# The first part of a fused attention and feed-forward kernel, rescheduled step by step

## The reference

```python
x = x + matmul(fake_quant(layernorm(x)), fake_quant(ctx))            # "L0": 8-bit levels, float result
x = x + ffn(layernorm(x))       # h @ W.T + b + LoRA mixed by a router over the mean of rows 179..510
x = x + attention(layernorm(x), ctx)     # 32 query heads, 8 key/value heads, rope, softmax, output product
x = x + ffn2(layernorm(x))      # h @ W_up.T + top-1 expert LoRA
```

## Time and profile before

| | |
|---|---|
| median of 3 runs | 2168.59 us (2164.77 to 2170.65) |
| the profiled execution | 2167.87 us, its span 2166.1 us |
| mean granted TensorE clock | 0.983 |
| busy share of the span | PE 95%, PEld 71%, DVE 72%, ACT 46%, POOL 37% |
| chain that ended last | PE 84%, DVE 7%, DMA 3%, issue 2% |

### The profile page before, as it was taken

One profiled execution on the slowest core, in us unless ns is written; L12 is line 12 of the kernel. 1 busy time (PEld: TensorE's weight loads), 2 busy tenths in 40 slices (PEclk: granted clock), 3 DMA queues, 4 the chain that ended last, 5 costly groups with the idle time before them and its releaser, 6 DMA issues.

```text
span 2166.1 us, 25646 instructions
## 1 busy us (share of the span) xinstructions
PE 2058.2 (95%) x9176; PEld 1539.6 (71%) x9176; DVE 1563.3 (72%) x2861; ACT 986.9 (46%) x1402; POOL 802.2 (37%) x521
## 2 busy tenths in 40 slices
PE   6999798899979999999999999999999999998799
PEld 5777575777846777777777777677777777776587
DVE  3874588646457888878888788778787878787343
ACT  3222122231146555555555555555565655556210
POOL 3445442560033434343434343343434343433300
PEclk9999999999989999999999999999999999999999
DMA  6443342343597887877868799887777786778321
GB/s 255 155 147 136 107 165 78 115 139 117 175 260 149 185 165 156 165 169 152 185 136 185 166 246 213 191 177 167 154 172 170 148 179 142 177 151 177 120 78 49
DMA packets 663454, 345.04 MB, mean 159 GB/s; under 512 B 575104, under 2 KB 599936, under 8 KB 660256
## 3 DMA queue, kind: packets, MB, share of 16 engines
q1 hardware_dynamic: 663328, 343.41, 65.5%
HBM read 154.60 MB, written 46.14 MB: 93 GB/s over the span
## 4 chain that ended last, share of the span: by engine, by line
PE 84%; DVE 7%; DMA 3%; issue 2%; ACT 1%; POOL 1%; SPq 1%; DVEq 0%; ACTq 0%
PE ps L43 27%; PE ps L45 27%; PE ps L44 27%; DMA pT<-pp 1%; PE ps L744 1%; DMA raw<-in_wv 1%; DVE t_sb L1065 1%; DVE raw L1097 1%; DVE tmp L1094 0%; DVE x_lo L1179 0%; PE ps L751 0%; DVE pp L1373 0%; POOL u_sb L1771 0%; DVE psb L1356 0%; SPq L551 0%
## 5 line engine op out<-in xcount | busy, mean ns | idle before, releaser
L1663 ACT ACTIVATE psb<-psb,st 128x1024 f32<-128x1024 f32 x256 | 295.2, 1153 | 230.7 <-DVE st L1359 230.7
L1373 DVE SCALAR_TENSOR_TENSOR pp<-psb,st,pp 128x1024 f16<-128x1024 f32 x256 | 386.7, 1511 | 3.1 <-ACT pp L1670 1.0
L1356 DVE CUSTOM_DVE_ANT_0 psb<-ps,mask 128x1024 f32<-128x1024 f32 x256 | 313.4, 1224 | 94.2 <-PE ps L45 89.4
L1670 ACT ACTIVATE pp<-psb,st 128x1024 f16<-128x1024 f32 x256 | 293.8, 1148 | 139.0 <-DVE st L1368 136.4
L1810 POOL TENSOR_TENSOR wol<-araw,woh 128x512 fp32r<-128x512 f32 x128 | 167.9, 1312 | 461.3 <-ACT woh L1621 461.3
L1810 POOL TENSOR_TENSOR wql<-araw,wqh 128x512 fp32r<-128x512 f32 x128 | 165.3, 1291 | 325.0 <-ACT wqh L1621 325.0
L43 PE MATMUL ps<-woh,osb 128*128 128x512 f32 x512 | 202.7, 396 | 14.9 <-DVE xa L1065 9.2
L43 PE MATMUL ps<-slots,wl 128*128 128x512 f32 x448 | 180.3, 402 | 33.4 <-issue 22.8
L43 PE MATMUL ps<-ksb,qsb 128*128 128x512 f32 x512 | 201.4, 393 | 10.5 <-DVE st L1356 6.3
L1065 DVE TENSOR_TENSOR xa<-ps,xa 128x512 f32<-128x512 f32 x256 | 175.5, 686 | 46.9 <-PE ps L45 46.9
L43 PE MATMUL ps<-pT,vsb 128*128 128x512 f16 x512 | 197.2, 385 | 9.7 <-DMA pT<-pp 9.6
(11 more groups left out here) (241 smaller groups left out, 4167.1 us busy)
## 6 DMA issues: line engine op xcount, KB each, us to landing
araw<-in_wq SPq DMA_DIRECT2D x128, 256.0 KB, 4.7
araw<-in_wo SPq DMA_DIRECT2D x128, 256.0 KB, 4.4
k_scratch<-khl SPq DMA_DIRECT2D x32, 512.0 KB, 3.6
ksb<-k_scratch SPq DMA_DIRECT2D x16, 1024.0 KB, 6.1
raw<-in_wk SPq DMA_DIRECT2D x16, 512.0 KB, 5.4
raw<-in_ctxT SPq DMA_DIRECT2D x16, 512.0 KB, 3.7
raw<-in_wv SPq DMA_DIRECT2D x16, 512.0 KB, 4.6
v_scratch<-vhl_sb SPq DMA_DIRECT2D x32, 256.0 KB, 2.7
```

The costliest lines, as they stand in the source:

```text
L1356: e.tensor_tensor_reduce(out=psb[:, n % 3, :], in0=pair(n % 2 * 2), in1=mask[:, i, :], scale=1.0, scalar=LOWEST, op0=ALU.add, op1=ALU.max, ...
L1373: e.scalar_tensor_tensor(out=pp[:, r, 1024:2048], in0=psb[:, r, :], scalar=st[:, n // 4 % 4, 16 + i:17 + i], in1=pp[:, r, 0:1024], op0=ALU ...
L1663: e.activation(P, P, ACT.Exp, bias=c[:, 4 + i:5 + i], accum_out=c[:, 8 + i:9 + i]).then_inc(a_exp.sem, 1)
L1670: e.activation(pp[:, r, 0:1024], psb[:, r, :], ACT.Copy, scale=st[:, n // 4 % 4, 16 + i:17 + i]).then_inc(a_ph.sem, 1)
```

## The change

Only the order of work in the first part changes, and who does a part of it:

1. `RAW` has another order and other slots: context tiles for L0 use slot 2 only; w tiles alternate. SP loads w(s//2+2) at an even step s, a step pair earlier than before.
2. Low parts: 13 even w tiles stay on GpSimd, all the others (45 of 58) are on VectorE; before, VectorE had 7 and GpSimd 51.
3. `KS` and `VS` change places (values first); in the groups of four, the second pair of halves runs one k-tile behind the first (`group_order`).
4. The places of `x_norm`, `x_quantise`, `c_quantise`, `a_turn`, L0, `ffn_norm` and `ffn_turn` are given by tables. L0 goes to steps 24 and 53 and uses three PSUM banks. The first feed-forward tile is turned at step 56.
5. c9 to c15 and c16 to c23 are split in smaller portions, partly before the group or product that needs them.
6. In the feed-forward, sums for the router are taken tile by tile (`row_sums`), and products, transpositions and layer norms of the tiles are interleaved in another order; `ffn_end` on VectorE is parted into `ffn_add` and `h_norm`. The first four wq loads are issued before the h stores.

```diff
-LO_ON_DVE = ["c0", "c1", "c3", "c5", "c7", "w2", "w18"]
-LO_ON_POOL = [key for key in SPLIT_ORDER if key not in LO_ON_DVE]
+LO_ON_POOL = [f"w{n}" for n in range(4, 32, 2) if n != 18]
+LO_ON_DVE = [key for key in SPLIT_ORDER if key not in LO_ON_POOL]
-KS = [s for s in range(64) if s // 2 % 2 == 0]
-VS = [s for s in range(64) if s // 2 % 2 == 1]
+KS = [s for s in range(64) if s // 2 % 2 == 1]
+VS = [s for s in range(64) if s // 2 % 2 == 0]
+L0_BANKS = [7, 4, 5]
+FFN_BANKS = [[0, 1], [2, 6], [3, 4]] + [[0, 1], [2, 3]] * 2 + [[0, 1]]
...
+    def group_order(group):
+
+        if len(group) == 1:
+            return [(k, s) for k in range(8) for s in group]
+        first, second = group[:2], group[2:]
+        out = [(0, s) for s in first]
+        for k in range(1, 8):
+            out += [(k, s) for s in first] + [(k - 1, s) for s in second]
+        return out + [(7, s) for s in second]
...
+    X_NORM_AT = {0: 0, 8: 1, 12: 2, 16: 3, 25: 4, 36: 5, 40: 6, 44: 7}
+    X_QUANTISE_AT = {6: 0, 10: 1, 14: 2, 18: 3, 26: 4, 38: 5, 42: 6, 46: 7}
+    A_TURN_AT = {9: 0, 14: 1, 18: 2, 22: 3, 29: 4, 41: 5, 45: 6, 50: 7}
+    C_LOAD_AT = {4: 1, 6: 2, 8: 3, 10: 4, 12: 5, 14: 6, 16: 7, 20: 8, 24: 9, 38: 11, 40: 12, 42: 13, 44: 14, 46: 15}
+    C_QUANTISE_AT = {0: 0, 5: 1, 7: 2, 9: 3, 11: 4, 13: 5, 15: 6, 17: 7, 25: 8, 27: 9, 37: 10, 39: 11, 41: 12, 43: 13,
+                     45: 14, 47: 15}
+    L0_AT = {24: 0, 53: 1}
+    FFN_NORM_AT = {49: 0, 55: 1, 57: 2, 59: 3}
+    FFN_TURN_AT = {56: 0, 59: 1}
...
@@ sync_program
-            if s % 2 == 0 and s < 62:
-                load_raw(f"w{s // 2 + 1}")
+            if s % 2 == 0 and s < 60 and n not in (14, 15):
+                load_raw(f"w{n + 2}")
...
@@ l0_product
-                if n < 2:
-                    e.wait_ge(v_ctab.sem, v_ctab[b, n])
-                else:
-                    e.wait_ge(v_l0.sem, v_l0[b, n - 2, 0])
+                if n in (1, 2):
+                    e.wait_ge(v_ctab.sem, v_ctab[b, n - 1])
+                elif n:
+                    e.wait_ge(v_l0.sem, v_l0[b, n - 3, 0])
...
@@ vector_program, the loop over steps
+                if s % 4 == 3 and s < 62 or s == 61:
+                    split_lo(f"w{s // 2 + 2}")
...
@@ vector_program, after the loop
+        h_norm(6)
         h_lo(5)
-        ffn_end(6, [0, 1])
+        ffn_add(7)
+        h_norm(7)
         h_lo(6)
-        ffn_end(7, [2, 3])
         h_lo(7)
@@ gpsimd_program
+                if s % 4 == 1 and s % 32 > 1 and s < 60:
+                    split_lo(f"w{s // 2 + 2}")
```

More of the change, by code:

```diff
@@ L296, in steps @@
                 yield [s]
-    def halves_done(s):
[L300 to L309, removed]
+    def group_order(group):
[6 more added lines that the diff above has]
+        return out + [(7, s) for s in second]
+    def halves_done(s):
+        return [s - 2, s - 1] if s % 4 == 2 else []
+    X_NORM_AT = {0: 0, 8: 1, 12: 2, 16: 3, 25: 4, 36: 5, 40: 6, 44: 7}
[7 more added lines that the diff above has]
+    FFN_TURN_AT = {56: 0, 59: 1}
+    BIAS_AT = {56: 0, 57: 1, 60: 2, 61: 3}
     quantised = []
     for n in range(64):
[L314 to L319, removed]
+        if n in C_QUANTISE_AT:
+            quantised.append(("x", C_QUANTISE_AT[n]))
+        if n in X_QUANTISE_AT:
+            quantised.append(("a", X_QUANTISE_AT[n]))
     h_tiles = [("h", i) for i in range(8)]
@@ L464, in sync_program @@
         load("sink", sink[:, :])
+        load("scal", scal[:, 0:4])
+        load_raw("w2")
+        load_raw("x0")
+        load_raw("w3")
+        for i in range(4):
+            e.dma_start(x_tile(i), A["x"][i]).then_inc(d_x[i].sem, 16)
         load("identf", identf[:, :])
@@ L603, in sync_program @@
         load_h(0, 2)
-        for n in range(3, 6):
+        for n in range(4, 6):
             load_w(("q", n))
@@ L1277, in vector_program @@
             s = group[0]
[L1278 to L1279 removed]
             for r in halves_done(s):
                 v_end(r)
+            if s in L0_AT:
+                l0_end(L0_AT[s])
             if s == 32:
[L1283 to L1285 removed]
+                for c in range(12, 16):
+                    split_lo(f"c{c}")
             if len(group) > 1:
                 split_lo("w2" if s == 0 else "w18")
[L1288 to L1289 removed]
@@ new lines, in vector_program @@
+            if s in X_NORM_AT:
+                x_norm(X_NORM_AT[s])
+            if s in C_QUANTISE_AT:
+                c_quantise(C_QUANTISE_AT[s])
+            if s in X_QUANTISE_AT:
+                x_quantise(X_QUANTISE_AT[s])
+            if s - 1 in FFN_TURN_AT:
+                ffn_lo(FFN_TURN_AT[s - 1])
+            if s in FFN_NORM_AT:
+                ffn_norm(FFN_NORM_AT[s])
+        split_lo("c19")
+        row_sums(1)
+        split_lo("w33")
+        split_lo("c20")
+        ffn_lo(2)
@@ L1313, in vector_program @@
+        split_lo("c21")
+        split_lo("c22")
+        ffn_lo(3)
+        split_lo("c23")
+        row_sums(2)
+        router(0)
+        ffn_norm(4)
+        router_end(0)
+        ffn_norm(5)
         lora_scale(0)
-        ffn_end(0, [0, 1])
-        ffn_end(1, [2, 3])
+        ffn_add(0)
+        ffn_add(1)
+        ffn_add(2)
         ffn_lo(4)
-        h_lo(0)
-        ffn_end(2, [0, 1])
         ffn_norm(6)
-        h_lo(1)
         ffn_lo(5)
-        h_lo(2)
+        row_sums(5)
+        ffn_add(3)
@@ new lines, in scalar_program @@
+            if s in X_NORM_AT:
+                root(("x", X_NORM_AT[s]))
+            if s - 1 in X_QUANTISE_AT:
+                row_sum(X_QUANTISE_AT[s - 1])
+            if s - 1 in FFN_TURN_AT:
+                ffn_hi(FFN_TURN_AT[s - 1])
+            if s in FFN_NORM_AT:
+                root(("f", FFN_NORM_AT[s]))
+        split_hi("w33")
+        split_hi("c20")
+        split_hi("c21")
+        ffn_hi(2)
+        split_hi("c22")
+        split_hi("c23")
+        ffn_hi(3)
+        root(("f", 4))
@@ L1605, in scalar_program @@
+        router_exp(0)
+        root(("f", 5))
         lora_hi(0)
-        for c in range(19, 24):
-            split_hi(f"c{c}")
         def split_w(key):
```

533 lines of the change are left out of this document (264 added, 269 removed), and 9 rows, old and new, of the table RAW.

## The result

The changed kernel takes 2153.05 us (median of 6 runs, 2146.44 to 2157.19) against 2167.36 (2164.77 to 2170.65) for the kernel before: a ratio of 0.9929, 95% interval 0.991 to 0.9947, so 15.4 us faster by the ratio. 2134 was predicted, with a range that ended at 2150. The direction is right, the size is not: less than half of the forecast gain is there.

What follows compares the result with a forecast made beforehand. TensorE was taken as the bound only where stretches hold little besides halves, with VectorE equally followed in quantising steps. Terms -2.5 - 4.4 - 3.8 - 32.8 + 10.0 = -33.5 gave 2134 us, range 2108 to 2150.

Steps and rivals of the forecast that it cites:

- Start: 0 to 35.14 us: first low parts done earlier on VectorE, w2's low part begun before the group ends; -2.5 us.
- Halves 4 to 23: 35.14 to 160.90 us: earlier loads remove SP's gaps, VectorE's lateness leaves 9.0 us of waits and 1 for clock; -4.4 us.
- the four predicted places: Before halves 10, 14, 18 and 22: TensorE gaps of 2 to 3 us, released by VectorE's low part of the weight.
- the rival in which VectorE keeps pace: Waits from 4 to 23 and in the second batch vanish, with half the feed-forward's 9.9 us; 2118 us, chance 0.27.
- The price of a round: VectorE's time for four quantising halves: 24.1 us of pieces plus 0.2 for meeting GpSimd, 24.3 against 22.3 for TensorE.
- the low part behind a rope: In each quantising round on VectorE: 1.29 us waiting for GpSimd's addition plus 1.07, priced at 2.4 us.
- The rival that put VectorE harder bound: GpSimd's 2.4 us low parts fall into the quantisations each time, +3 us in six rounds; 2152 us, chance 0.14.
- L0 and the second group: 160.90 to 250.42 us: three banks remove L0's inner waits, 1.5 us put for late context tiles; -3.8 us.
- each arrives 0.6 to 1 us early: In the second group: c9 to c15, passing through three slots, come before TensorE needs them; 1.5 us put for misses.
- 250 to 459: 250.42 to 459.33 us: gaps before L0 and at a turn, clock loss and moved work leave it; 176.1 against 208.91, -32.8 us.
- Feed-forward: 459.33 to 603.08 us: 134.0 work, 9.9 new waits, 7.5 for the last load, 2.4 clock; 153.8 us, +10.0.
- The shift is carried to the end: Behind 603.08 us: the heads start the same way from the last load, so the total of -33.5 us reaches the end.

Runs made afterwards that it cites:

- sum_first: Changed kernel with ScalarE taking the row sums of quantised row tiles ahead of the rounding of the second key half; 2152.51 us, ratio 0.992.
- low_on_pool: Changed kernel with twelve low parts of odd w tiles moved back from VectorE to GpSimd; 2141.42 us, ratio 0.9876.
- c_first: Changed kernel with w33, c20 and c21 loaded ahead of the stores of halves 62 and 63; 2145.81 us, ratio 0.9893.
- lo_first: Changed kernel with the low part of h tile 6 ahead of tile 7's layer norm (ScalarE's high part ahead of its root); 2150.78 us, ratio 0.9917.
- tail_order: Changed kernel with x tile 7 stored ahead of two wq loads, and h tile 6 stored behind the last load of h; 2150.59 us, ratio 0.9916.
- after_again: The changed kernel unedited, timed and profiled once more; 2151.73 us, ratio 0.9926.
- mix_late_h7: mix with x tiles 4 and 5 stored earlier, two wq loads and last h stores later, h tile 7's high and low parts behind the first ropes; 2129.79 us.
- mix: Changed kernel with the edits of low_on_pool, sum_first, c_first and tail_order together; 2133.8 us, ratio 0.9838.
- low_on_vector: Changed kernel with ten more low parts moved from GpSimd to VectorE, which then has 55 of 58; 2144.91 us, ratio 0.9892.
- the last kernels: mix_late_h7, and it with x's layer norms behind the second value half and two wq loads ahead of h tile 6's store; ratios 0.9821 and 0.9809.

## Why the prediction was wrong, point by point

Against the profiled execution before the forecast was -33.5 us, and -19.4 was measured in the profile. By its own terms:

- *Start:* -1.6 (half 4 at 33.50) for -2.5.
- *Halves 4 to 23:* -1.5 (125.76 to 124.22) for -4.4. The waits were put at 9.0 us and are 7.5; in sum_first, with the turn's gap out of the way, they are 8.1 in the four predicted places and 1.1 before half 8. The turn's wait for ScalarE's row sum was not foreseen (the rival in which VectorE keeps pace took it for removed), but cost nothing on its own. The rest is the clock: in the window 72.91:98.03 it is 0.92 and 103 matmuls take what 116 take in the next. **The price of a round was the weak point.** 24.3 us were walked; 25.12 are there. The 0.2 us "for now and then meeting one of GpSimd's 2.4 us low parts" is 2.17 in each round, always on the same operation; the other pieces were about 1.1 us too dear (24.1 for 25.12 - 2.17). Most of that is the low part behind a rope, priced at 2.4 us: it takes 1.23 in every round, and it is GpSimd's addition that takes 2.32 for its 1.29 (the lines in low_on_pool). The two do exclude each other, as the prediction had it, but GpSimd is the one that waits, so the 2.4 us did not stand. The quantisation behind it was put at 3.5 and takes 4.1, as it meets GpSimd twice and not once. The rival that put VectorE harder bound had this kind of mechanism, though on the quantisations and at +3 us a round where 0.8 came. That its 2152 us lies beside the 2153 measured is luck: most of the miss lies elsewhere.
- *L0 and the second group:* -1.7 for -3.8. L0 runs without inner gaps (17.5 us) as said, but "each arrives 0.6 to 1 us early" failed: TensorE waited 3.58 and 0.49 us in the group. The second pair's w17 has its low part behind that of c10 on VectorE, and c10's load was issued at 216.92 us, behind two stores of values.
- *250 to 459:* -33.1 for -32.8. This term stands; it carries the gain. The gaps of 7.0, 6.5 and 4.4 us of the earlier trace rows stood there and are gone, and one of 2.31 has come; but no run parts the gain among the items of the change, so how it divides is argued and not shown.
- *Feed-forward:* +14.8 for +10.0. This is **the step that failed most**, in three terms: waits in it 11.9 instead of 9.9, where c20 (2.81, from SP's order by c_first) and the turn of h tile 6 (2.29) were missing and the other turns cost less than said; waits for hTb 9.5 instead of 7.5; work with its clock 137.1 instead of 136.4. The mechanism named for the end was wrong. It was said that the chain starts 5.7 us later since `h_lo(6)` stands behind the norm of tile 7. The size was right: the last store of x is issued 10.9 us after the end of the products, 5.0 before. The cause was not: lo_first put the low part ahead again and won nothing in the stretch. What the runs show in its place is SP's order and the stores' time to land: ScalarE may write the high part of h tile 5 only when tile 4's store has landed (6.56 us, the line at 551.91), which makes the turn of tile 6 late; and the last store of x is issued behind a load of h, two wq loads and four stores, at 568.44, and takes 6.39 us where it took 4.17 in the earlier trace rows. Two runs bear this out: the earlier store of x in tail_order took 5.8 us from the wait for hTb against after_again, and the earlier stores of x tiles 4 and 5 in mix_late_h7 took away the gap at the turn of tile 6.
- *"The shift is carried to the end":* the last load comes 23.3 us earlier than before, the end 19.4. The query products run at the lower clock behind the gap of 7.75 us, which takes 2.5, of which 1.3 have come back by 637 us. From there to the change of the batch element another 2.5 are lost, 1.4 of them in waits for pT between 1247 and 1292 us (0.52, 0.49, 0.73 for one of 0.32 before).
- *Profile and median:* the changed kernel's runs spread over 10.8 us, and the profiled one lay 4.5 below the median. Before, profile and median were 0.7 apart. This is the last part of the miss, and the range left no room for it.

In sum 2134 failed by three small terms of the same sign (0.9, 2.9, 2.1), the feed-forward (4.8), the heads (3.9) and the spread (4), less 0.3 of the third stretch.

The predicted time was there to be had by further edits: mix is at 2133.8 and mix_late_h7 at 2129.8, with some dozen lines of the changed kernel edited.

What stays open: why the same store of x takes 6.4 us instead of 4.2; why the heads take back nothing of a shift in one execution and much in another (after_again: the last load 16.6 us earlier than before, the end 16.6; low_on_vector: 24.7 and 16.9, with waits for pT of 0.3 to 2.0 us from 1247 us on), and the 7 to 8 us at the third score in the last kernels.

## What to carry to other kernels

Price a move between VectorE and GpSimd by the instruction that it will meet, and not by its own length alone: here a GpSimd instruction of 2.4 us cost a full VectorE 2.2 us when it fell on the norm's SBUF-to-SBUF operation, and nothing when it fell on maxima that read PSUM. Two experiments that go in opposite directions (more, and less, of the same work) tell a load from a meeting; one alone would have confirmed a theory that is half right. And before a gap is priced, look at the period of the engine behind it: if that repeats exactly, only what shortens the period counts.

## What the runs showed of the hardware

- A VectorE operation with one SBUF input (the norm's last, 128x1024) took 2.98 us beside a GpSimd low part of 2.39 us, 0.81 without. By the records it began 0.05 us *ahead* of GpSimd's (126.67 and 126.72), and waited all the same.
- A VectorE low part (two SBUF inputs) that began 0.05 us ahead of GpSimd's addition took its full speed, 1.23 us; the addition took 2.32 us, 1.29 elsewhere (92.76 and 92.81). So the start times in the records do not tell which of the two will wait.
- Two maxima out of PSUM beside the same work: 1.28 us, as without it; GpSimd's low part took 2.84 instead of 2.39 there, from the end of a quantisation on.
- A store of 512 KB took 6.39 us at the end of the feed-forward, behind a load of 1 MB and other stores, against 4.17 us before.
